# Two load pieces of w1 issued from ACT's queue instead of the sync queue, in a gated FFN with quantized weights

## What is computed

```python
x = x + tanh(g_xattn) * (0.6 * sigmoid(si[:, :, None] + sj[:, None, :] + b) + 0.4 * layernorm(x))   # si, sj = ctx @ W halves
def bitlinear(x, w):
    xn = x * rsqrt(mean(x * x) + 1e-6)
    xq = round(xn * 127 / max|xn|) (and back)          # per row
    wq = clip(round(w / mean|w|), -1, 1) * mean|w|     # one mean over the whole weight
    return xq @ wq.T
h = layernorm(x)
x = x + tanh(g_ffn) * bitlinear(silu(bitlinear(h, w1)) * bitlinear(h, w2), w3)
```

## Time and profile before

| | |
|---|---|
| Runs: median of 3 (lowest to highest) | 155.48 us (155.3 to 155.5) |
| The profiled execution's own time | 154.29 us |
| Its span | 152.5 us |
| PE busy | 137.5 us, 90% of the span |
| DVE busy | 118.8 us, 78% |
| POOL busy | 107.6 us, 71% |
| ACT busy | 103.8 us, 68% |
| Granted TensorE clock | 1.0 |

### The profile page before, as it was taken

One profiled execution on the slowest core, in us unless ns is written; L12 is line 12 of the kernel. 1 busy time (PEld: TensorE's weight loads), 2 busy tenths in 40 slices (PEclk: granted clock), 3 DMA queues, 4 the chain that ended last, 5 costly groups with the idle time before them and its releaser, 6 DMA issues.

```text
span 152.5 us, 2380 instructions
## 1 busy us (share of the span) xinstructions
PE 137.5 (90%) x711; PEld 75.6 (50%) x711; DVE 118.8 (78%) x179; ACT 103.8 (68%) x172; POOL 107.6 (71%) x158
## 2 busy tenths in 40 slices
PE   1379568989999999799999999999999999999992
PEld 1279557955554444344444444445454454444461
DVE  0235998999999999979999999992779468908742
ACT  3148599999989778977597794283919719572250
POOL 3021297999898489894998969999742985699420
PEclk9999999999999999999999999999999999999999
DMA  4899999996129569980469519255802195819773
GB/s 122 229 409 406 410 407 426 404 384 217 34 71 142 129 149 237 204 158 21 78 130 232 94 37 141 63 152 149 198 2 89 43 185 111 232 69 227 184 217 138
DMA packets 46004, 27.94 MB, mean 183 GB/s; under 512 B 37543, under 2 KB 37928, under 8 KB 45992
## 3 DMA queue, kind: packets, MB, share of 16 engines
q1 hardware_dynamic: 45696, 27.79, 68.1%
q10 hardware_dynamic: 296, 0.01, 0.1%
HBM read 14.55 MB, written 4.20 MB: 123 GB/s over the span
## 4 chain that ended last, share of the span: by engine, by line
PE 72%; ACT 11%; DMA 6%; issue 5%; POOL 3%; ACTq 1%; SPq 1%; DVE 1%; DVEq 0%; POOLq 0%
PE ps L1404 42%; PE ps L1441 23%; ACT junk L720 3%; DMA th_ring<-in_L_xattn_b_dram 3%; DMA xqT<-xq 2%; POOL hq L587 2%; PE ps L1436 2%; ACT w2T L725 1%; PE ps L1310 1%; ACT w1T L730 1%; ACT th_ring L775 1%; ACT junk_x L792 1%; ACT raw_room L805 1%; PE ps L1317 1%; ACT hqT L736 1%
## 5 line engine op out<-in xcount | busy, mean ns | idle before, releaser
L1404 PE MATMUL ps<-w1T,xqT 128*128 128x512 f16 (+1 forms) x192 | 40.7, 361 | 0.9 <-DMA xqT<-xq 0.9
L1404 PE MATMUL ps<-w2T,xqT 128*128 128x512 f16 (+1 forms) x192 | 40.7, 362 | 0.0
L1125 DVE SCALAR_TENSOR_TENSOR raw<-ps,deq,raw_room 128x1408 f32<-128x1408 f32 x16 | 26.9, 1683 | 14.2 <-PE ps L1404 14.1
L1441 PE MATMUL ps<-w3T,hqT 128*128 128x512 f16 x165 | 37.2, 379 | 0.3 <-issue 0.3
L805 ACT ACTIVATE raw_room<-ps,deq 128x1408 f32<-128x1408 f32 x16 | 22.9, 1433 | 14.9 <-PE ps L1404 14.9
L1404 PEld LDWEIGHTS ps<-w1T,xqT 128*128 128x128 f16 x192 | 18.6, 98 | 20.9 <-issue 1.6
L1404 PEld LDWEIGHTS ps<-w2T,xqT 128*128 128x128 f16 x192 | 18.3, 98 | 20.1 <-DVE raw L1125 1.2
L1132 DVE TENSOR_REDUCE h_top<-raw 128x1 f32<-128x1409 f32 x16 | 25.7, 1607 | 0.1
L587 POOL TENSOR_SCALAR hq<-raw,h_scale 128x1408 f16<-128x1408 f32 x15 | 22.6, 1506 | 4.4 <-DVE h_scale L1135 4.4
L1441 PEld LDWEIGHTS ps<-w3T,hqT 128*128 128x128 f16 x165 | 16.1, 98 | 19.0 <-issue 0.7
L816 ACT ACTIVATE junk<-raw 128x1410 f16<-128x1410 f32 x16 | 21.8, 1368 | 0.0
(11 more groups left out here) (106 smaller groups left out, 180.2 us busy)
## 6 DMA issues: line engine op xcount, KB each, us to landing
c_all<-in_x_dram SPq DMA_DIRECT2D x16, 256.0 KB, 10.0
out_dram<-out_ring SPq DMA_DIRECT2D x15, 256.0 KB, 2.5
raw<-in_L_ffn_w_dram SPq DMA_DIRECT2D x4, 704.0 KB, 12.7
raw_room<-in_L_ffn_w_dram SPq DMA_DIRECT2D x3, 768.0 KB, 8.6
raw<-in_L_ffn_w_dram SPq DMA_DIRECT2D x3, 768.0 KB, 11.7
hq<-in_ctx_dram SPq DMA_DIRECT2D x2, 256.0 KB, 6.2
raw_room<-in_L_ffn_w_dram SPq DMA_DIRECT2D x1, 512.0 KB, 10.7
raw<-in_L_ffn_w_dram SPq DMA_DIRECT2D x1, 512.0 KB, 11.7
```

The lines of the kernel that those rows point to most:

```text
L1125: v.scalar_tensor_tensor(out=hid[:, t % HS, 0:H], in0=ps_up[:, 0:H], scalar=deq[:, 1, t:t + 1], in1=gate[:, t % GATES, :], op0=ALU.mult, o ...
L1404: last = m.matmul(bank[:, lo:hi], xqT[:, i % XT, k, :], wT[w][:, k, lo:hi], start=(k == 0), stop=(k == KD - 1))
L1441: last = m.matmul(ps_y[t % 2], hqT[:, t % HT, k, :], w3T[:, :, k, :], start=(k == 0), stop=(k == KH - 1))
```

## The change

SP's list loses the loads of pieces 0 and 1 of w1. ACT gets a `load_w` of its own and issues the two pieces behind its four row loads and ahead of its first activation (with the table load that this brings).

```diff
             load_ctx(0)
             load_x(0)
-            load_w(0, 0)
-            load_w(0, 1)
             load_w(0, 2)
             load_w(0, 3)
             load_x(1)
...
+            def load_w(w, k):
+                lo, hi = PIECES[w][k]
+                act.dma_start(raw[w][:, lo:hi, :], w_t[w][:, lo:hi, :]).then_inc(w_in[w][k], 16)
...
                 act.dma_start(row[0:1, lo:lo + src.shape[1]], src).then_inc(row_in, 16)
+            load_w(0, 0)
+            load_w(0, 1)
             act.wait_ge(consts, 1)
             s.activation(junk_x[:, 1, 0:1], ones[:, 0:1], ACT.Silu).then_inc(gates_th, 1)
```

## The result

| | before | changed |
|---|---|---|
| Median of the runs (lowest to highest) | 155.49 us (155.30 to 155.72) | 157.86 us (157.49 to 158.87) |
| Ratio | | 1.0162, 95% interval 1.0108 to 1.0216 |
| The profiled execution, its span | 154.29, 152.5 us | 158.23, 156.4 us |
| PE busy | 137.5 us | 137.2 us |
| Last instruction on DVE starts at | 149.69 us | 152.41 us |

The kernel is slower by 2.4 us in the medians; 157.5 us was predicted. PE did the same work. The two profiled executions differ by 3.9 us, but 1.2 us of that lies behind DVE's last instruction: it starts 2.72 us later, and the span ends 2.3 us after its end before and 3.5 us after it here.

What follows compares the result with a forecast made beforehand. PE was taken as the bound after about 33 us, so early lateness reaches the end. Terms 0 + 0 + 0 + 2.5 - 0.15 - 0.4, about +2.0 us, gave a median of 157.5 us, range 155.3 to 158.8.

Steps and rivals of the forecast that it cites:

- The new bound: At DVE's first sum of w1: piece 1 lands past its slack (11.6 us) and makes intercept(0) late by 2.5 us.
- The landing of piece 1: On ACT's queue beside SP's loads: 14.2 us, between order of issue (13.9) and equal halves (14.5); 10.7 before.
- more than forecast: Rival: piece 0 also behind pieces 2 and 3, or ACT's issues 1.2 us each; +3.3, 158.8 us; chance 0.04.
- The start of intercept(0): On DVE, behind its first sum of w1: 15.4 us instead of 12.86, +2.5.
- What DVE takes up behind it: Slack on DVE after intercept(0): 0.15 us at scale_w(0), 0.4 at two waits for PE; +2.0 left at evac_rows(8).
- ACT's two issues: Ahead of ACT's table load: 0.49 us each, at most 1.2; ctx_out(0) moves to about 5.0, hidden by 3.2 us of cover.
- SP's two issues less: On SP's queue: issues of 0.43 and 0.49 us go away, worth nothing by itself as SP is not late.
- Piece 0: At ACT's first sum of w1: lands near 10.6 us instead of 8.75; first tanh 0.2 late, not the longest way.
- The landing of the row: Small row loads on ACT's queue, b last: landing left at 6.70 us, up to 2 us of disturbance hidden.
- The dip and its cure: Faster rival: two queues fill the engines from 3 to 6 us, at most 0.9 us won, 154.6 us; chance 0.08.
- No change: Rival: ACT's queue is served so that piece 1 lands by 11.6 us, time 155.5 us; chance 0.10.
- The path from the first product on: PE is full from the first gate product on, so the +2.0 us there arrives unchanged at the end.

Runs made afterwards that it cites:

- the run with piece 0 alone: The changed kernel with only piece 0 of w1 on ACT's queue and pieces 1, 2 and 3 on SP; ratio 1.0112 to the kernel before.
- the control: The kernel before, with DVE's sum of piece 1 moved behind intercept(0) and make_x(0); ratio 1.0091.
- the run with piece 1 alone: The changed kernel with only piece 1 of w1 on ACT's queue and pieces 0, 2 and 3 on SP; ratio 0.9993 to the kernel before.
- the loads all on SP: The kernel before, still with all w1 loads on SP, but pieces 2 and 3 issued ahead of 0 and 1; ratio 1.0202, median 156.84 us.
- the swap: The changed kernel with the two pieces on ACT's queue in the other order, piece 1 ahead of piece 0; ratio 1.0378 to the kernel before.
- the hold: The changed kernel with one wait added: SP issues piece 2 only when piece 0 has landed; ratio 1.0313 to the kernel before.
- the second version with b on SP: The kernel before, with b loaded by SP between x(0) and piece 0, and DVE's copy of the spread row ahead of stats_x(0); ratio 1.0018.
- ACT's issues without traffic: The kernel before plus two small loads (2 KB in all) issued on ACT behind the row loads into spare room; ratio 1.0226, profiled execution 153.85 us.
- the first version with b on SP: The kernel before, with the load of b issued by SP between x(0) and piece 0 instead of last on ACT; ratio 1.0034.

## Why the prediction was right, and where it was off

- *The new bound.* Right: piece 1's landing at DVE's sum, with the waits for it shown there and nowhere else on the chain. The forecast of +2.0 us stands against 2.4 in the medians and 2.7 in DVE's last instruction. That 157.5 came within 0.4 us of the measured 157.86 says less than the landing times do: the same change gave 1.0281 on another chip, where its median was 158.02 and that of the kernel before 155.19, and 3.1 us in DVE's last instruction.
- *The landing of piece 1*, 14.2 taken between 13.9 and 14.5: mis-sized; 14.9 measured, above both ends and next to the 15 of the rival *more than forecast*, to which I had given 0.04. Equal halves are right from 7 us on (1.24 and 1.16 MB up to 13 us). What I left out is that the sharing does not begin with both queues level: from 4.5 to 7 us SP's queue moved 0.51 MB and ACT's 0.11. SP's piece 2 was issued 0.5 us before piece 0 (1.64 and 2.16); whether that is the reason, and whether it makes up all of the 0.4 us above 14.5, no run shows. The rule that I had put beside it (the Trainium skill, "DMA: Bandwidth & Descriptors", "Queues, rings and completion order": each DMA engine takes the queues with work in turn) gave 14.5 and was nearer. The bytes from 7 to 13 us agree with it; those from 4.5 to 7 us are not equal.
- *The start of intercept(0)*: 15.4 forecast, 16.07 measured, +3.2 instead of +2.5, all of the difference from the landing.
- *What DVE takes up behind it*: 0.15 at scale_w(0) and 0.4 at two later waits. Measured: 0.2 at scale_w(0) (+2.97), 0.4 more up to the second w_tot (+2.55), and then +2.85 at evac_rows(8). The last step, from the second w_tot to evac_rows(8), went the other way, since DVE's clip of quantized w1 tiles (L1109, 128 x 1536) took 1.02 us (at 34.32) instead of 0.56; in the second profile of the change it did not, and evac_rows(8) was at 36.02, +2.2.
- *ACT's two issues*: 0.49 each was right (0.46 and 0.51), and ctx_out(0) moved to 4.75, far inside its cover. SP's two issues less were worth nothing.
- *Piece 0* at 10.6: 11.2, so the first tanh was 0.7 late and not 0.2. Hidden here; the run with piece 0 alone shows its price.
- *The landing of the row*, left at 6.70: PE started on it at 5.88 and 6.02 in the two profiles of the change, which was hidden as well. I had called a row that lands much before 6.7 a sign of being wrong. It is none: the control has the loads of the kernel before and its row was in by 5.33. I can't say what sets it; see below.
- *The dip and its cure*, the faster rival: the dip stayed. *No change* would have needed piece 1 by 11.6; the run with piece 1 alone (11.9) was nearly that case, and its ratio is 0.9993.
- *The path from the first product on*, taken as full, so that lateness arrives at the end unchanged: right to 0.4 us in eight of the thirteen other profiles, and off by 0.9 to 2.2 us in the other five; see below.

## What to carry to other kernels

When the DMA engines are full, moving a load to another queue gains no bandwidth (402 GB/s with two heavy queues here, 408 with one); it changes the order of landing. So ask for every load which instruction stands at it and how long it may stand, before asking which engine issues it. A load with little slack should have nothing heavy beside it on any queue, and a wait early in an in-order list costs all that is queued behind it.

## What the runs showed that I had not expected

**DVE and POOL hold each other up by whole instructions.** I compare, in every profile, by how much the first gate product ends later than before (35.41) and by how much DVE's last instruction starts later. In eight the two agree to 0.4 us: among them the first profile of the change (2.85 and 2.72), the loads all on SP (1.83 and 1.84) and the swap (4.46 and 4.46). In five the end is later than the first product explains: the hold by 2.2 us, DVE's control by 1.6, pieces 2 and 3 on ACT by 1.35, the second version with b on SP by 1.3, and the second profile of the change by 0.9. Every profile has a make_x of 2.0 to 2.3 us on DVE between 77 and 83 us; these five, and no others, have one more, of 2.5 to 3.4 us, before 50 us. The second version with b on SP:

```profile
34.32 2.35 POOL L578 TENSOR_TENSOR hqT<-out_ring,w_wide 128x1024 f32<-128x1024 f32 x1
...
34.53 3.22 DVE L1034 SCALAR_TENSOR_TENSOR c_all<-th_ring,t,c_all 128x1024 f32<-128x1024 f32 x1
...
42.15 2.55 PE L1404 MATMUL ps<-w2T,xqT 128*128 128x512 f16 x12 [1.83 <-DVE raw L1125]
```

The kernel before:

```profile
34.74 1.27 DVE L1034 SCALAR_TENSOR_TENSOR c_all<-th_ring,t,c_all 128x1024 f32<-128x1024 f32 x1
34.88 1.18 POOL L513 TENSOR_TENSOR x_step<-x_top,rnorm 128x1 f32<-128x1 f32 x1
...
36.02 2.36 POOL L577 TENSOR_TENSOR hqT<-out_ring,w_wide 128x1024 f32<-128x1024 f32 x1
```

The same instruction of DVE takes 1.27 us when it starts before POOL's work, and then POOL's little x_step takes 1.18 us (0.19 in the other kernel). It takes 3.22 us when POOL's product of 2.35 us began 0.21 us before it, and PE then waits 1.83 us for DVE. In the hold (3.41 us) and the control (3.38 us) it is the same pair. (Spans on POOL are rough in this profile.) The second profile of the change shows it at another meeting, and pieces 2 and 3 on ACT has the same rows (1.73 and 2.46 us):

```profile
47.60 1.73 POOL L564 TENSOR_SCALAR w3q<-raw,w_scale 128x1408 f16<-128x1408 f32 x1
...
47.94 2.46 DVE L1038 SCALAR_TENSOR_TENSOR c_all<-th_ring,t,c_all 128x1024 f32<-128x1024 f32 x1
```

In the first profile of the change this make_x took 1.27 us, beside a POOL conversion of 2.94 us: the same kernel, the other way round. Here the starts do not tell which of the two gives way: POOL's conversion starts before make_x in both profiles (47.91 and 48.35 in the first), with a clip by DVE beside it (at 47.92 in the first, at 47.50 in the second). The Trainium skill, "SBUF — State Buffer", section "SBUF: two separate sides", states it: a DVE operation with two SBUF inputs and a GpSimd operation that reads SBUF lock a pair of ports against each other for the whole instruction. The rows of make_x and of POOL's product agree. So a shift of a few tenths at the start can cost or save 1 to 2 us later, which fits the scatter of these runs; that it makes up the scatter was not tested.

**The granted clock fell to half, and no row shows a cost.** In the first profile of the change PE stood idle for 3.7 us until 19.3; the granted clock is 1.00 up to 16 us and 0.50, the level of 1.2 GHz, from 18 us to about 31 us. The windows of the changed kernel (the granted clock is the third number from the end):

```profile
14.00:16.00 2.00, 0.72 (x5) 0.42 (x4) 1.06 (x1) 1.87 (x7) 0.00 (x0) 1.00 1.05 408
...
18.00:20.00 2.00, 0.67 (x3) 0.70 (x4) 1.97 (x5) 0.00 (x0) 0.00 (x0) 0.50 1.05 410
```

Four transposes of ctx(1) took 1.09 us at this level and 1.09 us at full clock in the kernel before (17.54 us there). It was back at 1.00 from 32 us on, before the products started. The two profiles with the earliest ends (ACT's issues without traffic, and the first version with b on SP) have the same fall.

**The row's landing varies, and not with the loads alone.** PE started on the spread row at 6.74 before the change, at 5.88 and 6.02 in the two profiles of the change, and anywhere from 4.79 to 6.99 in the other kernels that left the row loads on ACT, with and without a second heavy queue. With b's load on SP it was 4.49 and 4.47. DVE's control has the same loads in the same order as the kernel before, and there it was 5.33. What sets it in the dip between 3 and 6 us stays open. It matters for the comparison: the only profile of the kernel before has a late row, which holds intercept(0) until 12.86, while with the pieces of w1 in the same place and an earlier row (ACT's issues without traffic: 5.58) it starts at 12.06. Against that the lateness of the change is 4.0 us and not 3.2. Whether this is a reason for the larger ratios on the later chips was not tested.
